# Routed expert layers on one core: the second layer of a tile two tiles behind its first, transposes two ahead, a whole PSUM bank per tile

## The chip, the cores and the metric

One core of a Trainium2 chip runs the whole program. The metric is the device time of one execution in microseconds (us). TensorE is PE in the profile, VectorE DVE, ScalarE ACT, GpSimd POOL, SyncE SP.

## What is computed

Two stages over 8192 tokens of 128 features, all in float32. The first is a graph layer (normalise, multiply with the adjacency, two dense layers, add the input). The second, which the change is about, sends each token to the best two of 8 experts:

```python
gate_logits = xf @ Wg + bg
top_w, top_i = jax.lax.top_k(gate_logits, TOP_K)      # TOP_K = 2
top_w = jax.nn.softmax(top_w, axis=-1)
w_dense = jnp.sum(jax.nn.one_hot(top_i, E) * top_w[..., None], axis=1)
for e in range(E):                                    # E = 8, D = 128, H = 512
    h = jax.nn.gelu(xf @ W1[e] + b1[e], approximate=False)
    out = out + w_dense[:, e:e + 1] * (h @ W2[e] + b2[e])
x = x + out                                           # xf is the layernorm of x
```

## The kernel before

Tokens are handled in 16 groups of 512 in the graph stage. As groups finish, POOL writes their rows with indirect DMAs (`dispatch`, L495) to two tables in HBM, sorted by expert, one table for the first choice and one for the second. The expert stage then walks over 142 tiles of 128 rows: 71 tiles of first choices (`TILES`), then 71 of second choices (`NT` is 142). Each tile belongs to one expert, whose number and first row stand in small tables that the engines read into registers.

The program is written out engine by engine, and every engine runs its own list in order; semaphores are the only link. For tile i:

- **SP** loads the tile's rows from HBM to place i % 16 of `slot_rows` (`load_slots`, L390 or L393), once the write of tile i - 16 has landed (`added`). From tile 79 on the rows come from the table `forwarded`, to which the first-choice tiles were written; SP first waits until the writes of all first-choice tiles have landed (L436). For the eight second-choice tiles 71 to 78, which are loaded earlier, it loads the first-choice result apart (`load_prior`, L399), two such loads behind each of the loads of tiles 79 to 82.
- **DVE** normalises the rows (`norm_slots`, L1134, `AHEAD` = 4 tiles ahead of the tile it closes), copies the expert's first-layer weights and biases to place i % 4 of `block_w` (`copy_block`, L1128, 128x644, three tiles ahead), and closes a tile: it adds the output bias to PE's result (L1219; L1229 for second choices) and multiplies by the token's weight and adds (L1223; L1237).
- **PE** turns the normalised rows (`turn`, a transpose, L720), does layer 1 (four 128x128 products, L727) and layer 2 (four products summed in one bank, L742).
- **ACT** copies the turned rows to SBUF (`copy_slots`, L858) and applies the gelu to the four pieces of layer 1 (`gelu`, L864).
- **POOL** writes the closed rows back with an indirect DMA (`write_tile`: L507 to `forwarded` for first choices, L511 to the output for second choices). It is also the engine that raises variances to the power -1/2 for the last group (L484) and that dispatches its rows.

PE's order in iteration i is turn(i + 1), layer 1 of i, layer 2 of i - 1. Layer 1 of a tile fills halves of PSUM banks: two pieces in a bank, three banks in rotation (`FH_BANKS`), so that the three banks hold one tile and a half. ACT starts the gelu of the first two pieces when the first half is done:

```python
for c in range(C):                                            # layer1(i), PE
    after(pe, gelu_ready, 2 * (2 * i + c // 2 - FH_BANKS + 1))
    ...
act.wait_ge(fh_done, 2 * i + c // 2 + 1)                      # gelu(i), ACT
```

`turn` and layer 2 have two banks each (`TURN_BANK`, `Y_BANK`), `slot_t` and `gelu_t` two buffers each. Layer 2 of tile i waits for the bias addition of tile i - 2 (`y_chain`), which empties its bank. The small steps that finish the last group (statistics of the second norm, gate, ranks, tables for the late tiles) are laced into the first 17 iterations of DVE's list.

## Time and profile before

| | |
|---|---|
| median of 3 runs | 521.77 us (519.33 to 522.0) |
| profiled execution, span | 521.4 us |
| PE busy | 473.0 us, 91% |
| DVE, ACT, POOL busy | 343.4, 302.9, 271.9 us |
| 142 transposes of the expert stage | first at 205.16 us, last at 510.59 us |

A line of the profile names the engine, the line of the kernel, the operation, what it writes and reads, the number of instructions merged in the line and, in square brackets, how long the engine had stood idle before it and what ended that wait. PE counts each float32 product of 128x128 as two matmuls, so layer 1 and layer 2 of a tile are 8 matmuls each; a transpose is one. "PEclk" is the granted clock of PE as a share of 2.4 GHz, 0.5 being its lower level of 1.2 GHz.

### The profile page before, as it was taken

The page shows a single profiled execution, that of the slowest core. Times are in us where ns is not written, and L with a number is a line of the kernel's source. Part 1 is how long each engine was busy: PE and PEld are TensorE (multiplying, and loading weights), DVE is VectorE, ACT ScalarE, POOL GpSimd, SP SyncE. Part 2 cuts the span into 40 slices and gives each one's busy share as a digit, 9 for nine tenths or more (in the row PEclk, how much of TensorE's full clock was granted, in tenths as well). Part 3 has the DMA queues.
Part 4 walks back from the last instruction along what each step waited for, and adds up shares of the span by engine and source line. Part 5 has one row for each costly group of instructions (what it writes and reads, how often), then busy time and mean ns, then how long its engine had stood idle before and what let it go on. Part 6 is the DMA issues. An engine that isn't in the chain of part 4 may idle for free.

```text
span 521.4 us, 13855 instructions
## 1 busy us (share of the span) xinstructions
PE 473.0 (91%) x3585; PEld 418.1 (80%) x3585; DVE 343.4 (66%) x1438; ACT 302.9 (58%) x942; POOL 271.9 (52%) x276
## 2 busy tenths in 40 slices
PE   8999989889988986869698999899997999999995
PEld 5678666667766755869697999899987999999995
DVE  5777767779766765556656666666645666677673
ACT  4475545556554333645455766677755766777663
POOL 3325556568666665356555454445435544455544
PEclk9999999999999989789899999999998999999999
DMA  7993333322222222134333433333044433334210
GB/s 213 375 312 99 97 85 78 77 78 69 67 69 79 71 75 69 39 96 121 93 102 100 126 118 116 114 86 110 20 120 124 137 96 102 109 109 107 84 36 12
DMA packets 50835, 54.61 MB, mean 105 GB/s; under 512 B 10249, under 2 KB 39474, under 8 KB 50760
## 3 DMA queue, kind: packets, MB, share of 16 engines
q1 hardware_dynamic: 42048, 35.14, 25.7%
q0 software_dynamic: 8240, 18.29, 10.1%
q8 instruction: 34, 0.56, 0.5%
q14 instruction: 41, 0.34, 0.3%
q10 hardware_dynamic: 472, 0.29, 0.2%
HBM read 33.56 MB, written 21.52 MB: 106 GB/s over the span
## 4 chain that ended last, share of the span: by engine, by line
PE 66%; issue 12%; POOL 8%; another core or an unknown queue 6%; DVE 4%; ACT 3%; POOLq 0%; DVEq 0%; ACTq 0%
PE ps L727 25%; PE ps L742 25%; PE ps L647 5%; POOL dispatched_rows L495 4%; PE ps L720 3%; PE ps L633 2%; PE ps L607 2%; ACT gelu_t L864 2%; POOL powers L484 1%; POOL powers L476 1%; PE ps L640 1%; PE ps L597 1%; POOL out_y L511 1%; ACT hidden L790 1%
## 5 line engine op out<-in xcount | busy, mean ns | idle before, releaser
L864 ACT ACTIVATE gelu_t<-ps,block_w 128x128 f32<-128x128 f32 x568 | 164.4, 374 | 49.1 <-PE ps L727 37.2
L727 PE MATMUL ps<-slot_t,block_w 128*128 128x128 f32 x1136 | 155.8, 281 | 13.6 <-ACT slot_t L858 10.8
L742 PE MATMUL ps<-experts,gelu_t 128*128 x1136 | 156.0, 281 | 11.0 <-ACT gelu_t L864 8.2
L727 PEld LDWEIGHTS ps<-slot_t,block_w 128*128 128x128 f32 x1136 | 142.6, 196 | 15.4 <-ACT slot_t L858 12.0
L742 PEld LDWEIGHTS ps<-experts,gelu_t 128*128 128x128 f32 x1136 | 141.9, 196 | 15.1 <-issue 15.0
L511 POOL DMA_INDIRECT out_y<-slot_rows x71 | 69.7, 981 | 74.4 <-DVE slot_rows L1237 40.1
L507 POOL DMA_INDIRECT forwarded_rows<-slot_rows x71 | 71.1, 1002 | 71.6 <-DVE slot_rows L1223 41.5
L495 POOL DMA_INDIRECT dispatched_rows<-payload,row_idx x80 | 82.6, 1032 | 24.8 <-issue 22.2
L633 PE MATMUL ps<-agg_r,w1b 128*128 128x512 f32 x128 | 62.7, 619 | 13.4 <-ACT hidden L790 10.8
L1128 DVE COPY block_w<-experts 128x644 f32 x142 | 72.9, 513 | 1.3 <-issue 1.3
L858 ACT COPY slot_t<-ps 128x128 f32<-128x128 f32 x142 | 38.1, 269 | 59.4 <-PE ps L720 36.5
L647 PE MATMUL ps<-w2e,hidden 128*128 128x136 f32 x512 | 67.5, 279 | 0.0
L647 PEld LDWEIGHTS ps<-w2e,hidden 128*128 128x128 f32 x512 | 63.0, 190 | 0.0
L1219 DVE TENSOR_TENSOR y_bias<-ps,block_w 128x128 f32<-128x128 f32 x71 | 20.7, 291 | 58.2 <-PE ps L742 35.5
L633 PEld LDWEIGHTS ps<-agg_r,w1b 128*128 128x128 f32 x128 | 22.5, 194 | 42.9 <-issue 20.5
L1229 DVE TENSOR_TENSOR slot_rows<-ps,block_w 128x128 f32<-128x128 f32 x71 | 20.7, 291 | 49.8 <-PE ps L742 27.6
L1134 DVE TENSOR_SCALAR slot_n<-slot_rows 128x128 f32<-128x128 f32 x142 | 49.8, 352 | 1.8 <-issue 1.4
L790 ACT ACTIVATE hidden<-ps,vec_cols 128x512 f32<-128x512 f32 x64 | 41.7, 689 | 10.0 <-PE ps L633 9.1
L720 PE MATMUL ps<-ident,slot_n 128*128 128x128 f32 x142 | 39.1, 276 | 0.0
L476 POOL TENSOR_TENSOR powers<-powers_in,neg_half 128x4 f32<-128x4 f32 x15 | 16.7, 1114 | 38.4 <-DVE powers_in L927 38.4
L484 POOL TENSOR_TENSOR powers<-powers_in,neg_half 128x8 f32<-128x8 f32 (+1 forms) x16 | 23.2, 1449 | 22.4 <-DVE powers_in L954 22.4
L640 PEld LDWEIGHTS ps<-ident_wg,xs_t 128*128 128x128 f32 x128 | 20.6, 190 | 14.3 <-issue 14.3
(152 smaller groups left out, 458.7 us busy)
## 6 DMA issues: line engine op xcount, KB each, us to landing
slot_rows<-forwarded_rows SPq DMA_DIRECT2D x63, 131.0 KB
slot_rows<-dispatched_rows SPq DMA_DIRECT2D x79, 67.0 KB
xs<-in_x SPq DMA_DIRECT2D x16, 256.0 KB, 6.9
xs_t<-in_x_t SPq DMA_DIRECT2D x16, 256.0 KB, 6.1
experts<-in_f_w SPq DMA_DIRECT2D x16, 256.0 KB, 5.2
slot_rows<-rrms_rows SPq DMA_DIRECT2D x13, 256.0 KB
adj_in<-in_adj_t SPq DMA_DIRECT2D x16, 128.0 KB, 6.5
dispatched_rows<-payload,row_idx POOLq DMA_INDIRECT x80
```

The costliest lines, as they stand in the source:

```text
L495: pool.indirect_dma_start(rows[k], bass.IndirectOffsetOnAxis(row_idx[:, g, j * TOP_K + k:j * TOP_K + k + 1], 0), payload[:, g * JT + j, 0: ...
L507: pool.indirect_dma_start(forwarded, place, slot_rows[:, r, :], None, bounds_check=DUMMY - 1, oob_is_err=False).then_inc(added[r], 16)
L511: pool.indirect_dma_start(out, token, slot_rows[:, r, WID:FWD], None, bounds_check=T - 1, oob_is_err=False).then_inc(added[r], 16)
L633: pe.matmul(bank(n % H_BANKS, 0, GROUP), w1b[:, c * P:(c + 1) * P], agg_r[:, s % 2, :], start=True, stop=True).then_inc(h_done, 1)
L647: mm = pe.matmul(x2_part(j), hidden[:, c, j * P:(j + 1) * P], w2e[:, c, :], start=False, stop=(c == C - 1))
L720: pe.transpose(bank(TURN_BANK + i % 2, 0, P), slot_n[:, i % (AHEAD + 1), :], ident[:]).then_inc(slots_turned, 1)
L727: mm = pe.matmul(bank((2 * i + c // 2) % FH_BANKS, c % 2 * SLOTS, SLOTS), block_w[:, i % BLOCKS, c * P:(c + 1) * P], slot_t[:, i % 2, :], ...
L742: mm = pe.matmul(bank(Y_BANK + i % 2, 0, P), gelu_t[:, i % 2, c, :], experts[:, bass.ds(at + (OW2 + c * P), P)], start=(c == 0), stop=(c = ...
L790: act.activation(hidden[:, c, :], ps[:, (C * s + c) % H_BANKS, :], ACT.Silu, scale=vec_cols[:, GRW + c:GRW + c + 1]).then_inc(hidden_ready, 1)
L864: act.activation(gelu_t[:, i % 2, c, :], ps[:, (2 * i + c // 2) % FH_BANKS, c % 2 * SLOTS:(c % 2 + 1) * SLOTS], ACT.Gelu, bias=block_w[:, ...
L1128: dve.tensor_copy(block_w[:, i % BLOCKS, :], experts[:, bass.ds(at, OW2)]).then_inc(block_ready, 1)
L1134: dve.tensor_scalar(slot_n[:, i % (AHEAD + 1), :], row[:, X2:WID], row[:, MEAN:MEAN + 1], row[:, RSTD:RSTD + 1], ALU.subtract, ALU.mult).t ...
```

## The change

- PE's order in iteration i becomes layer 1 of i, turn(i + 2), layer 2 of i - 2.
- Layer 1 of a tile goes to one whole bank, three tiles in three banks, with one wait before and one signal behind its four products; ACT waits for the whole tile before the first gelu. `slot_t` has 3 buffers (`TURNS`), `gelu_t` 4 (`GELUS`), laid over the room of `adj_in`, which the graph stage no longer needs.
- `AHEAD` is 6 and `BLOCKS` 6: rows are normalised six tiles ahead and weights copied five ahead.
- DVE's closing is split: the bias addition (`add_bias`, which empties the bank) comes first in an iteration, then the norm, the weight copy and the register load, and the multiplication by the weight (`close_first`, `close_second`) last. The steps for the last group move: its statistics go ahead of the loop, the others one to two iterations earlier.

```diff
-BLOCKS = 4
+BLOCKS = 6
-    AHEAD = 4
+    AHEAD, LAG, TURNS, GELUS = 6, 2, 3, 4
...
-        slot_t = sb("slot_t", [P, 2, SLOTS])
-        gelu_t = sb("gelu_t", [P, 2, C, SLOTS])
+        slot_t = sb("slot_t", [P, TURNS, SLOTS])
+        gelu_t = adj_in[:].rearrange("p r j n -> p (r j n)").rearrange("p (t c s) -> p t c s", t=GELUS, c=C)
...
             def layer1(i):
                 pe.wait_ge(slots_copied, i + 1)
                 pe.wait_ge(block_ready, i + 1)
+                after(pe, gelu_ready, C * (i - FH_BANKS + 1))
                 for c in range(C):
-                    after(pe, gelu_ready, 2 * (2 * i + c // 2 - FH_BANKS + 1))
-                    mm = pe.matmul(bank((2 * i + c // 2) % FH_BANKS, c % 2 * SLOTS, SLOTS),
+                    mm = pe.matmul(bank(i % FH_BANKS, c * SLOTS, SLOTS),
...
-                    if c % 2:
-                        mm.then_inc(fh_done, 1)
+                mm.then_inc(fh_done, 1)
...
-            layer1(0)
-            for i in range(1, NT):
+            for i in range(NT + LAG):
                 if i == LAST_RANKS:
                     prefix(G - 1)
-                if i + 1 < NT:
-                    turn(i + 1)
-                layer1(i)
-                layer2(i - 1)
-            layer2(NT - 1)
+                if i < NT:
+                    layer1(i)
+                if i + 2 < NT:
+                    turn(i + 2)
+                if i >= LAG:
+                    layer2(i - LAG)
...
             def gelu(i):
-                after(act, y_done, i - 1)
+                after(act, y_done, i - GELUS + 1)
+                act.wait_ge(fh_done, i + 1)
...
+            for i in range(4, AHEAD):
+                norm_slots(i)
+                copy_block(i - 1, expert_of(dve, i - 1))
+                if i == 4:
+                    stats2_of(G - 1)
+                    moments2_of(G - 1)
+            at = expert_of(dve, AHEAD - 1)
             for i in range(NT):
+                if i < TILES:
+                    add_bias(i, y_bias[:, i % 2, :])
+                else:
+                    add_bias(i, slot_rows[:, i % RING, X2:WID])
                 if i + AHEAD < NT:
                     norm_slots(i + AHEAD)
                 if TILES < i <= TILES + SECONDS:
                     dve.wait_ge(y_chain, i)
-                if i + 3 < NT:
-                    copy_block(i + 3, at)
+                if i + AHEAD - 1 < NT:
+                    copy_block(i + AHEAD - 1, at)
...
                 if i < TILES:
-                    finish(i)
-                else:
-                    take_second(i)
+                    close_first(i)
```

PE's list in the expert stage, one iteration, before (`slots_copied`, `gelu_ready` and `y_chain` are the semaphores of ACT's copies, ACT's gelus and DVE's bias additions):

```order
L720 MATMUL ps<-ident,slot_n 128x128 [waits slots_copied,slots_normed]
L727 MATMUL ps<-slot_t,block_w 128x128 [waits gelu_ready,block_ready,slots_copied]
L727 MATMUL ps<-slot_t,block_w 128x128 [waits gelu_ready] x3
L307 TENSOR_LOAD early_expert
L307 ISA x2
L742 ISA [waits y_chain,gelu_ready]
L742 MATMUL ps<-experts,gelu_t 128x128
```

and now:

```order
L728 MATMUL ps<-slot_t,block_w 128x128 [waits gelu_ready,block_ready,slots_copied]
L728 MATMUL ps<-slot_t,block_w 128x128 x3
L721 MATMUL ps<-ident,slot_n 128x128 [waits slots_copied,slots_normed]
L308 TENSOR_LOAD early_expert
L308 ISA x2
L742 ISA [waits y_chain,gelu_ready]
L742 MATMUL ps<-experts,adj_in 128x128
```

The transpose has moved behind layer 1, the waits inside layer 1 are gone, and `adj_in` is the room of `gelu_t`.

DVE's list from the end of the last but one group to the first tiles' closing, before (L946 is the statistics of the last group):

```order
L1009 CAST row_idx<-row_f 128x8
L307 TENSOR_LOAD early_expert
L307 ISA x2
L1134 TENSOR_SCALAR slot_n<-slot_rows 128x128 [waits slots_loaded4]
L1128 ISA
L1128 COPY block_w<-experts 128x644
L307 TENSOR_LOAD early_expert
L307 ISA x2
L1219 TENSOR_TENSOR y_bias<-ps,block_w 128x128 [waits y_done]
L1223 SCALAR_TENSOR_TENSOR slot_rows<-y_bias,slot_rows 128x128 [waits y_chain]
L946 BN_STATS stats<-payload 128x6 [waits x2_ready]
```

and now:

```order
L1129 COPY block_w<-experts 128x644
L947 BN_STATS stats<-payload 128x6 [waits x2_ready]
L947 BN_STATS stats<-payload 128x6 x3
L953 BN_AGGR payload<-stats 128x2 [waits ln2_chain]
L953 BN_AGGR payload<-stats 128x2 x3
L955 TENSOR_SCALAR powers_in<-payload 128x4 [waits ln2_chain]
L1135 TENSOR_SCALAR slot_n<-slot_rows 128x128 [waits slots_loaded5]
L308 TENSOR_LOAD early_expert
L308 ISA x2
L1129 ISA
L1129 COPY block_w<-experts 128x644
```

The statistics of the last group now stand ahead of the first wait for `y_done`, and one more norm and weight copy too.

## Rows read from the trace of the kernel before

**Rows 1.** The page: span; timeline, DVE before the first bias addition.
```profile
span 521.4 us, 13855 instructions
...
215.70 0.29 DVE L1219 TENSOR_TENSOR y_bias<-ps,block_w 128x128 f32<-128x128 f32 x1 [4.05 <-PE ps L742]
```

**Rows 2.** Stretches, transposes alone: from:to length, PE busy (xtransposes) PEld, PEclk, DMA.
```profile
223.00:242.40 19.40, 1.94 (x7) 0.97 (x7) 0.91 0.37 106
242.40:265.00 22.60, 2.06 (x7) 1.19 (x8) 0.85 0.34 98
265.00:285.80 20.80, 2.45 (x9) 1.23 (x9) 1.00 0.37 107
285.80:342.00 56.20, 7.36 (x27) 3.87 (x28) 1.00 0.40 116
342.00:389.40 47.40, 6.82 (x25) 3.59 (x26) 1.00 0.31 83
389.40:403.40 14.00, 1.24 (x4) 0.69 (x5) 0.88 0.42 117
403.40:510.50 107.10, 14.99 (x55) 7.86 (x56) 1.00 0.35 97
```

**Rows 3.** Timeline of one steady tile: start, duration, engine, line.
```profile
361.18 1.06 PE L727 MATMUL ps<-slot_t,block_w 128*128 128x128 f32 x8
361.27 0.29 DVE L1219 TENSOR_TENSOR y_bias<-ps,block_w 128x128 f32<-128x128 f32 x1 [0.56 <-PE ps L742]
361.38 0.27 ACT L858 COPY slot_t<-ps 128x128 f32<-128x128 f32 x1 [0.24 <-issue]
...
361.88 1.14 ACT L864 ACTIVATE gelu_t<-ps,block_w 128x128 f32<-128x128 f32 x4 [0.24 <-issue]
...
362.07 1.06 PE L742 MATMUL ps<-experts,gelu_t 128*128 x8
362.12 0.49 DVE L1128 COPY block_w<-experts 128x644 f32 x1
```

**Rows 4.** Waits of PE, 200 to 521 us: total, times, longest.
```profile
PE ps L727 <- ACT slot_t L858: 10.8, 5, 4.6
PE ps L742 <- ACT gelu_t L864: 8.2, 9, 2.3
```

**Rows 5.** Timeline around the stop at 229 us.
```profile
223.09 0.27 PE L720 MATMUL ps<-ident,slot_n 128*128 128x128 f32 x1
...
227.09 0.98 POOL L507 DMA_INDIRECT forwarded_rows<-slot_rows  x1 [0.30 <-issue]
229.15 0.29 DVE L1219 TENSOR_TENSOR y_bias<-ps,block_w 128x128 f32<-128x128 f32 x1 [5.89 <-remote]
229.19 0.27 ACT L858 COPY slot_t<-ps 128x128 f32<-128x128 f32 x1 [3.72 <-remote]
...
229.51 2.07 PE L727 MATMUL ps<-slot_t,block_w 128*128 128x128 f32 x8 [2.64 <-ACT slot_t L858]
```

**Rows 6.** Timeline, POOL's power for the last group.
```profile
219.23 1.08 POOL L484 TENSOR_TENSOR powers<-powers_in,neg_half 128x4 f32<-128x4 f32 x1 [6.10 <-DVE powers_in L954]
```

**Rows 7.** Timeline of PE, the stop at 257 us.
```profile
257.73 2.07 PE L742 MATMUL ps<-experts,gelu_t 128*128 x8 [2.27 <-ACT gelu_t L864]
```

**Rows 8.** Timeline from the last first-choice tile to the tiles that wait for it.
```profile
374.12 0.98 POOL L507 DMA_INDIRECT forwarded_rows<-slot_rows  x1 [0.92 <-DVE slot_rows L1223]
...
377.26 0.34 SPq L393 DMA_DIRECT2D slot_rows<-forwarded_rows  x1
...
380.43 0.34 DVE L1134 TENSOR_SCALAR slot_n<-slot_rows 128x128 f32<-128x128 f32 x1
...
391.53 1.24 PE L727 MATMUL ps<-slot_t,block_w 128*128 128x128 f32 x8 [1.75 <-ACT slot_t L858]
```

**Rows 9.** Timeline near the end: a closing and its write, no weight copy between.
```profile
515.57 0.35 DVE L1237 SCALAR_TENSOR_TENSOR slot_rows<-slot_rows 128x128 f32<-128x128 f32 x1
516.71 0.98 POOL L511 DMA_INDIRECT out_y<-slot_rows  x1 [0.74 <-DVE slot_rows L1237]
```

More of the change, by code:

```diff
@@ L741, in layer2 @@
                 for c in range(C):
-                    mm = pe.matmul(bank(Y_BANK + i % 2, 0, P), gelu_t[:, i % 2, c, :],
+                    mm = pe.matmul(bank(Y_BANK + i % 2, 0, P), gelu_t[:, i % GELUS, c, :],
                                    experts[:, bass.ds(at + (OW2 + c * P), P)],
@@ L856, in copy_slots @@
                 act.wait_ge(slots_turned, i + 1)
-                after(act, fh_done, 2 * (i - 1))
-                act.copy(slot_t[:, i % 2, :], ps[:, TURN_BANK + i % 2, 0:SLOTS]).then_inc(slots_copied, 1)
+                after(act, fh_done, i - TURNS + 1)
+                act.copy(slot_t[:, i % TURNS, :], ps[:, TURN_BANK + i % 2, 0:SLOTS]).then_inc(slots_copied, 1)
             def gelu(i):
-                after(act, y_done, i - 1)
+                after(act, y_done, i - GELUS + 1)
+                act.wait_ge(fh_done, i + 1)
                 for c in range(C):
-                    act.wait_ge(fh_done, 2 * i + c // 2 + 1)
-                    act.activation(gelu_t[:, i % 2, c, :],
-                                   ps[:, (2 * i + c // 2) % FH_BANKS, c % 2 * SLOTS:(c % 2 + 1) * SLOTS], ACT.Gelu,
+                    act.activation(gelu_t[:, i % GELUS, c, :],
+                                   ps[:, i % FH_BANKS, c * SLOTS:(c + 1) * SLOTS], ACT.Gelu,
                                    bias=block_w[:, i % BLOCKS, OB1 + c:OB1 + c + 1]).then_inc(gelu_ready, 1)
             copy_slots(0)
+            copy_slots(1)
             for i in range(NT):
@@ L871, in _ @@
                     tanh(G - 1)
-                if i + 1 < NT:
-                    copy_slots(i + 1)
+                if i + 2 < NT:
+                    copy_slots(i + 2)
                 gelu(i)
@@ L1214, in _, with add_bias, close_first @@
                     early_counts(1)
[L1216 to L1217 removed]
+            def add_bias(i, into):
                 dve.wait_ge(y_done, i + 1)
[L1219 removed]
+                dve.tensor_tensor(into, ps[:, Y_BANK + i % 2, 0:P],
                                   block_w[:, i % BLOCKS, OB2:OB2 + P], ALU.add).then_inc(y_chain, 1)
+            def close_first(i):
                 dve.wait_ge(y_chain, i + 1)
[L1222 removed]
+                row = slot_rows[:, i % RING, :]
                 dve.scalar_tensor_tensor(row[:, WID:FWD], y_bias[:, i % 2, :], row[:, WEIGHT:WEIGHT + 1],
                                          row[:, X2:WID], ALU.mult, ALU.add).then_inc(y_ready, 1)
[L1226 to L1230 removed]
             def close_second(i):
```

45 lines of the change are left out of this document (16 added, 29 removed).

## The prediction

> **What bounds the kernel now.** I read four views. The stretches of the expert stage, with the transposes alone, count tiles, one transpose each. From 342.0 to 389.4 us there are 25 tiles in 47.4 us, 1.896 us each, with no time lost [rows 2]. The timeline of such a tile shows why: layer 1 starts at 361.18, layer 2 0.89 us later, and 2 x 0.89 plus 0.11 for the transpose is 1.896 [rows 3]. PE is the bound there and no buffer can make that tile faster. The change removes no work from PE. So all that it can win is the time by which the other stretches exceed 1.896 us a tile:
>
> - 223.0 to 242.4: 7 tiles, 19.4 - 13.3 = 6.1 us
> - 242.4 to 265.0: 7 tiles, 9.3 us
> - 265.0 to 285.8: 9 tiles, 3.7 us
> - 285.8 to 342.0: 27 tiles, 5.0 us
> - 389.4 to 403.4: 4 tiles, 6.4 us
> - 403.4 to 510.5: 55 tiles, 2.8 us
>
> The sum is 33.3 us [rows 2], 6% of the span of 521.4 us [rows 1]. That is the ceiling.
>
> The waits of PE say what ended its idle time: nearly all of it is ACT, with the copy of the turned rows (10.8 us in 5 waits, of which 4.6 lie before the first tile) and with the gelu (8.2 us in 9) [rows 4]. But ACT is not short of time: in a steady tile it works 0.27 + 1.14 us of 1.896 [rows 3]. The timeline around one stop shows what it waited for. The transpose of 223.09 is over at 223.36 by its record, but ACT copies it at 229.19, and DVE starts the bias addition of the layer 2 before it at 229.15; both had been idle for 3.7 and 5.9 us [rows 5]. So PE's signals reached two engines some 6 us late, and together. I call this a late signal. In this trace it comes while POOL issues indirect DMAs in a row, 0.30 us apart, and ends about 1 us behind the last of them (227.09 + 0.98, then 229.15) [rows 5]. I take the coincidence as it stands; what the change must do is bridge the late signals.
>
> **How late a signal may be, before and now.** Three paths lead from PE over another engine back to PE. From the steady tile [rows 3]:
>
> - Gelu: layer 1 starts at 361.18, its gelus end at 361.88 + 1.14 = 363.02, and layer 2 of the same tile starts 0.89 + 0.89 + 0.11 + 0.89 = 2.78 us after 361.18, at 363.96. A signal may be 0.9 us late. Now two more blocks of 0.89 and a transpose lie between, 1.9 us. But the first gelu waits for the whole tile; I take half of layer 1's length, 0.5 us, for that. Room: 2.3 us.
> - Transpose: it runs 0.11 us before 361.18, its copy ends at 361.65, and layer 1 needs it one tile later, at 363.08. Room 1.4 us. Now it stands behind layer 1 and is needed one block of 0.89 later: 2.3 us.
> - Bank of layer 2: it starts at 362.07; its bias addition is due at 361.27 + 1.90 = 363.17, ends at 363.46, and layer 2 of two tiles on needs the bank at 362.07 + 3.79 = 365.86. Room 2.4 us, and the same now: there are still two banks, and the addition stands first in DVE's iteration instead of behind the weight copy, which matters only when DVE is behind.
>
> So the shortest room rises from 0.9 to 2.3 us. **Each stop gets 1.4 us shorter**, and one shorter than that vanishes, with the refill behind it.
>
> **The sum.** Stretch by stretch, what stays of the excess:
>
> - 403.4 to 510.5 and 285.8 to 342.0: small stops; 7.8 us become 0.
> - 265.0 to 285.8: 3.7 become 1.0.
> - 242.4 to 265.0: the stop that ends at 257.73 is the largest of three (idle 2.27 us there alone [rows 7]), and PE stands at its lower clock behind it: PEclk 0.85 is a mean over 22.6 us, so 0.15 x 2 x 22.6 = 6.8 us were at 1.2 GHz [rows 2]. With two stops shortened by 1.4 us, and a third and half of the slow clock gone, 9.3 become 5.0.
> - 223.0 to 242.4: here the burst itself should go. POOL waited 6.10 us, until 219.23, for the last group's variance, dispatched two more blocks of rows, and only then wrote the first tiles in a row [rows 6, 5]. The statistics now stand ahead of DVE's loop, where DVE was idle for 4.05 us before 215.70 [rows 1]: some 6 us earlier, so that POOL is free when tile 0 is closed. 6.1 become 0.5.
> - 389.4 to 403.4: two stops, one of them 1.75 us [rows 8], shortened to about 2 us with refill. To that comes a price of the change. Tile 79 can be loaded only when tile 70 is written: write 374.12, load 377.26, norm 380.43 at the latest [rows 8]. From layer 2 of tile 70 to the transpose of tile 79 there were 7 tiles on PE; now there are 5 and a layer 1. And the closing of tile 70 stands behind the norm and the weight copy: from the start of the addition to the end of the copy DVE takes 361.27 to 362.61, 1.34 us [rows 3], of which the closing's 0.35 [rows 9] moves out, so it starts at 0.99 instead of 0.33, 0.66 us later. Tile 79 keeps some 0.5 us of room; tiles 80 to 84, whose loads share SP's queue with the eight loads of first-choice results, come up to 1 us late. 6.4 become 3.0, between 1 and 6.
>
> Together 9.5 of 33.3 us stay: a gain of 23.8 us. Edits at nothing: the extra norm and weight copy ahead of the loop (0.34 + 0.49 us) lie in DVE's 4.05 us idle [rows 1], without which the first tile would be closed 0.8 us later; the room of `gelu_t` and the third `slot_t` add no instruction. SP's loads keep room elsewhere: with 16 places and a norm 6 tiles ahead, ten tiles (19 us) lie between a closing and the norm that needs its place, and write, load and norm took 380.43 - 374.12 = 6.3 us in the narrowest place [rows 8]; before it was twelve tiles. The tail behind the last layer 2 is the same work. 521.4 - 23.8 = 497.6; the median of the runs shown is 0.4 us above the profiled execution, so I say **498 us**.
>
> A rule is weighed for the later closing. The Trainium skill ("SBUF — State Buffer", section "SBUF: two separate sides") says that while DVE copies float32 from SBUF to SBUF, GpSimd cannot write the descriptors of its DMAs. By it, a write behind the weight copy would start sooner after its closing than one ahead of it, and the later closing would cost about 0.1 us where I count 0.66. The trace does not show that: in a steady tile the write starts 0.8 us behind the closing with the copy in between, and at the end of the program, with no copy, it starts 0.79 us behind it (515.57 + 0.35, then 516.71) [rows 9]. I keep 0.66.
>
> **Rivals.**
>
> 1. *Long signals leave less.* If PE's stop is set by the end of the late signal and not by its start, the transpose and the bank decide in each long stop, and these gain 0.9 us and nothing. For it: in rows 5 both engines got their signals together. Then the stretches at 223, 242, 265 and 389 us give back about 9 us of 25.5, the small stops 7: 521.4 - 16 = 505. Chance 0.17.
> 2. *All of it is bridged*, the slow clock too, and the loads at tile 79 come in time: 521.4 - 33.3 = 488. For it, the stretch of 47.4 us at full rate [rows 2]. Chance 0.06.
> 3. *Nothing is bridged*: late signals last until POOL has no closed tile left, so a PE that runs on feeds them, and each grows by what the buffers give. 521.4, plus the 1 us at tile 79: 522. The Trainium skill ("Perfetto Trace Analysis", section "Optimization Strategy") ties a shortage of buffers to a gap that repeats from tile to tile; by that rule there is none here, since 25 tiles in a row show no gap. Chance 0.07.
> 4. *Slower: longer bursts.* During a late signal PE now finishes up to two tiles more. DVE then closes three in a row and POOL issues three or more DMAs 0.30 us apart, where it issued two. The run of writes that ended at 228.07 [rows 5] lies in the stretch that lost 6.1 us, some 3 us for each of its two stops. With some ten such places at +2 us each and the ceiling's small stops not recovered: 521.4 + 20 - 10 = 531. This decides from the point at which most of POOL's runs hold four DMAs or more. Against it: DVE closes a tile in no less than about 1.4 us (the steps of rows 3), POOL needs 1.28 a DMA, so POOL nearly keeps pace. Chance 0.06.
>
> The forecast's own case has 0.64: 490 to 504 us.
>
> **Numbers.** The smallest difference that runs of this kernel can tell is about 0.5%, 2.6 us. The range of 8 in 10 takes the forecast's case and the first rival and leaves out the other three: 490 to 512 us. Faster by over 0.5% (under 519.2): the forecast, rivals 1 and 2 and part of 3, 0.90. Within it 0.04; slower 0.06.
>
> **What would show it.** In the profile after: the same 1.896 us a tile in full stretches; PE's two large waits on ACT at 8 to 10 us together, the 4.6 ahead of the first tile among them, instead of 19.0; late signals on ACT and DVE still there, with PE running on; POOL's power for the last group near 213 us and no run of four writes behind it; the transposes of tiles 79 to 84 with up to 1 us of idle time, and DVE's norm there waiting for a load. It is wrong if those two waits stay above 15 us, if POOL's runs of four or more DMAs multiply, or if the tiles behind 79 lose over 5 us.

## Result, and the profile after

The kernel with the change took 527.43 us (median of 4 runs, 525.13 to 529.79), the kernel before 521.88 us (4 runs). The ratio is 1.0123, with a 95% interval of 1.0073 to 1.0172: slower by 1.2%, where 4.6% faster was forecast. The profiled execution of the changed kernel has a span of 523.8 us (521.4 before [rows 1]) and took 525.72 us. An execution more than 1.5% above the fastest of its kernel counts as slow; the ratios leave it out, the medians don't.

The stretches of the expert stage, transposes alone, in the kernel after (columns as in [rows 2]; the stretch from 212 to 223 us, which [rows 2] leaves out, held 5 transposes before):

```profile
212.00:223.00 11.00, 2.06 (x7) 1.12 (x7) 0.89 0.27 78
223.00:242.40 19.40, 2.88 (x11) 1.43 (x10) 1.00 0.40 114
242.40:265.00 22.60, 2.11 (x7) 1.12 (x7) 0.85 0.33 100
265.00:285.80 20.80, 2.73 (x10) 1.42 (x10) 1.00 0.37 110
285.80:342.00 56.20, 7.04 (x26) 3.56 (x25) 1.00 0.36 110
342.00:389.40 47.40, 6.33 (x23) 3.29 (x23) 1.00 0.29 82
389.40:403.40 14.00, 1.32 (x4) 0.70 (x4) 0.76 0.42 120
403.40:513.00 109.60, 14.91 (x55) 7.74 (x54) 1.00 0.34 92
```

Against [rows 2] it gains in two places: 11 tiles instead of 7 from 223 to 242, 10 instead of 9 from 265 to 286. It loses where I had no loss: 26 tiles in 56.2 us (6.9 us over 1.896 each, 5.0 before) and 23 in 47.4 us, the stretch that had run at full rate (3.8 us over, 0 before). From 389 to 403 us there are 4 tiles as before, now with the clock at 0.76 (0.88 before).

The waits of PE from 200 to 520 us (total, times, longest), which answer to [rows 4]:

```profile
PE ps L728 <- ACT slot_t L858: 7.4, 3, 3.6
PE ps L742 <- ACT adj_in L864: 7.0, 15, 0.5
PE ps L721 <- DVE slot_n L1135: 5.2, 3, 3.8
```

The first two fell from 19.0 to 14.4 us, the third is new, and the wait on the gelus is now 15 short ones instead of 9. (`adj_in` is the room in which `gelu_t` now lies.) Where these short waits come from shows in the timeline of six microseconds in the stretch that lost:

```profile
306.66 0.29 DVE L1220 TENSOR_TENSOR y_bias<-ps,block_w 128x128 f32<-128x128 f32 x1 [2.58 <-PE ps L742]
...
307.81 0.28 DVE L1220 TENSOR_TENSOR y_bias<-ps,block_w 128x128 f32<-128x128 f32 x1
...
308.69 0.98 POOL L508 DMA_INDIRECT forwarded_rows<-slot_rows  x1 [2.74 <-DVE slot_rows L1226]
...
309.31 0.29 DVE L1220 TENSOR_TENSOR y_bias<-ps,block_w 128x128 f32<-128x128 f32 x1 [0.29 <-PE ps L742]
...
309.97 1.14 POOL L508 DMA_INDIRECT forwarded_rows<-slot_rows  x1 [0.30 <-issue]
...
311.41 0.98 POOL L508 DMA_INDIRECT forwarded_rows<-slot_rows  x1 [0.30 <-issue]
...
312.00 1.06 PE L742 MATMUL ps<-experts,adj_in 128*128 x8
312.19 0.27 ACT L858 COPY slot_t<-ps 128x128 f32<-128x128 f32 x1 [2.89 <-PE ps L721]
...
313.03 0.29 DVE L1220 TENSOR_TENSOR y_bias<-ps,block_w 128x128 f32<-128x128 f32 x1 [2.49 <-remote]
...
314.48 1.15 PE L742 MATMUL ps<-experts,adj_in 128*128 x8 [0.42 <-DVE y_bias L1220]
...
315.06 0.98 POOL L508 DMA_INDIRECT forwarded_rows<-slot_rows  x1 [2.66 <-DVE slot_rows L1226]
```

PE's signals are late until 306.66 at DVE. It then adds the bias of three tiles at 306.66, 307.81 and 309.31, POOL writes them 0.30 us apart from 308.69 on, PE's next signals are late until 312.19 at ACT and 313.03 at DVE, and it begins again. From 306.66 to 313.03 are 6.37 us for three tiles, 2.12 us each instead of 1.896. This cycle of threes fills most of 286 to 361 us and 411 to 455 us. From 200 us on POOL issues 26 runs of three or more DMAs with less than 0.45 us between the end of one and the start of the next; before there were 10.

The last first-choice tiles and what waits for them, answering to [rows 8]:

```profile
375.38 0.34 SPq L394 DMA_DIRECT2D slot_rows<-forwarded_rows  x1
...
377.51 0.35 DVE L1135 TENSOR_SCALAR slot_n<-slot_rows 128x128 f32<-128x128 f32 x1 [1.15 <-DMA slot_rows<-forwarded_rows]
...
393.40 0.98 POOL L512 DMA_INDIRECT out_y<-slot_rows  x1 [0.30 <-issue]
395.51 0.29 DVE L1220 TENSOR_TENSOR slot_rows<-ps,block_w 128x128 f32<-128x128 f32 x1 [5.24 <-remote]
...
396.11 0.48 PE L721 MATMUL ps<-ident,slot_n 128*128 128x128 f32 x1 [3.84 <-DVE slot_n L1135]
```

The norm of tile 79 waits for its load, and behind that POOL issues a run of six, at whose end PE stands for 3.84 us.

What was gained and lost cancels inside the expert stage. From the second layer of tile 0 to that of tile 141 both traced executions take 300.5 us: the kernel after is 6.5 us ahead by tile 10 (19.2 us instead of 25.7) and 8.4 by tile 30, then loses 4.7 up to tile 70 (85.5 us for 40 tiles instead of 80.8) and 4.0 from tile 70 to 90. The spans differ by 2.4 us, 1.4 ahead of that stretch and 1.0 behind it. The medians differ by 5.5 us; the rest of that lies between executions and is in neither trace.

### The profile page after: what moved, and what is told of

The parts are those of the page before. It is cut to its first block, busy times and chain, and to the rows that moved or that the text cites. A ratio compares the mean times of both kernels' runs of the same rounds, so it can differ in the third digit from the quotient of the medians.

```text
span 523.8 us, 13856 instructions
## 1 busy us (share of the span) xinstructions
PE 473.2 (90%) x3585; PEld 416.1 (79%) x3585; DVE 330.8 (63%) x1438; ACT 289.7 (55%) x942; POOL 272.5 (52%) x276
## 4 chain that ended last, share of the span: by engine, by line
PE 55%; issue 16%; POOL 12%; another core or an unknown queue 6%; ACT 5%; DVE 4%; DMA 1%; SPq 0%; POOLq 0%; DVEq 0%; ACTq 0%
PE ps L742 21%; PE ps L728 20%; POOL dispatched_rows L496 7%; PE ps L721 5%; ACT adj_in L864 3%; PE ps L634 3%; POOL powers L477 2%; PE ps L648 2%; POOL powers L485 2%; PE ps L608 1%; PE ps L598 1%; DVE sum_sq L926 1%; PE ps L641 1%; DVE slot_n L1135 1%
## 5 line engine op out<-in xcount | busy, mean ns | idle before, releaser
L742 PE MATMUL ps<-experts,adj_in 128*128 x1136 | 155.4, 281 | 10.9 <-ACT adj_in L864 7.0
L864 ACT ACTIVATE adj_in<-ps,block_w 128x128 f32<-128x128 f32 x568 | 164.1, 387 | 1.3 <-PE ps L728 0.6
L742 PEld LDWEIGHTS ps<-experts,adj_in 128*128 128x128 f32 x1136 | 140.5, 195 | 17.1 <-issue 17.0
L508 POOL DMA_INDIRECT forwarded_rows<-slot_rows x71 | 72.7, 1024 | 74.5 <-DVE slot_rows L1226 50.5
L512 POOL DMA_INDIRECT out_y<-slot_rows x71 | 71.5, 1007 | 76.8 <-DVE slot_rows L1234 45.9
L496 POOL DMA_INDIRECT dispatched_rows<-payload,row_idx x80 | 79.8, 997 | 24.3 <-issue 22.2
L1129 DVE COPY block_w<-experts 128x644 f32 x142 | 70.5, 497 | 1.7 <-issue 1.5
L1220 DVE TENSOR_TENSOR y_bias<-ps,block_w 128x128 f32<-128x128 f32 x71 | 20.6, 290 | 63.5 <-PE ps L742 50.1
```

The costliest lines, as they stand in the source:

```text
L496: pool.indirect_dma_start(rows[k], bass.IndirectOffsetOnAxis(row_idx[:, g, j * TOP_K + k:j * TOP_K + k + 1], 0), payload[:, g * JT + j, 0: ...
L508: pool.indirect_dma_start(forwarded, place, slot_rows[:, r, :], None, bounds_check=DUMMY - 1, oob_is_err=False).then_inc(added[r], 16)
L512: pool.indirect_dma_start(out, token, slot_rows[:, r, WID:FWD], None, bounds_check=T - 1, oob_is_err=False).then_inc(added[r], 16)
L742: mm = pe.matmul(bank(Y_BANK + i % 2, 0, P), gelu_t[:, i % GELUS, c, :], experts[:, bass.ds(at + (OW2 + c * P), P)], start=(c == 0), stop= ...
L864: act.activation(gelu_t[:, i % GELUS, c, :], ps[:, i % FH_BANKS, c * SLOTS:(c + 1) * SLOTS], ACT.Gelu, bias=block_w[:, i % BLOCKS, OB1 + c ...
L1129: dve.tensor_copy(block_w[:, i % BLOCKS, :], experts[:, bass.ds(at, OW2)]).then_inc(block_ready, 1)
```

## The experiments

To read them together I count, in each profiled trace, the start of layer 2 of tile 0, the time from there to tile 70, from tile 70 to 90 and from tile 90 to 141, and POOL's runs of three or more DMAs less than 0.45 us apart, from 200 us on. At 1.896 us a tile the three stretches would take 132.7, 37.9 and 96.7 us (the last a little less, because no layer 1 stands between the second layers at the end). The kernel before was run beside every batch of experiments, and a ratio is always to it in the same batch.

| kernel | median, us | ratio (95%) | tile 0 at | 0-70 | 70-90 | 90-141 | runs of 3+ |
|---|---|---|---|---|---|---|---|
| before | 521.88 | | 214.0 | 157.6 | 44.3 | 98.6 | 10 |
| after | 527.43 | 1.0123 | 215.4 | 153.9 | 48.3 | 98.3 | 26 |
| e1 after, spaced | 509.82 | 0.9810 (0.9732-0.9889) | 215.3 | 144.9 | 45.5 | 94.8 | 1 |
| e2 order of before | 520.12 | 1.0043 (1.0008-1.0079) | 213.6 | 148.8 | 47.3 | 100.3 | 11 |
| e3 closing at once | 519.08 | 0.9982 (0.9933-1.0030) | 215.4 | 146.8 | 48.2 | 98.3 | 17 |
| e4 before, statistics early | 512.26 | 0.9880 (0.9815-0.9945) | 213.2 | 148.5 | 44.4 | 98.0 | 12 |
| e5 before, spaced | 513.12 | 0.9783 (0.9721-0.9846) | 215.5 | 150.8 | 42.4 | 95.8 | 2 |
| e6 before, in threes | 563.32 | 1.0747 (1.0684-1.0810) | 215.9 | 172.8 | 50.1 | 114.5 | 45 |
| e7 after, half the pause | 535.93 | none | 216.7 | 159.0 | 48.7 | 105.5 | 36 |
| e8 before, e4 + e5 | 511.02 | 0.9738 (0.9679-0.9797) | 216.3 | 147.4 | 44.1 | 95.8 | 1 |
| e9 e2, norms 4 ahead | 515.96 | 0.9868 (0.9792-0.9945) | 212.7 | 150.8 | 46.1 | 97.6 | 10 |
| e10 before, spread | 508.96 | 0.9743 (0.9682-0.9803) | 213.1 | 142.4 | 43.1 | 95.8 | 2 |
| e11 after, spread | 507.11 | 0.9730 (0.9667-0.9793) | 214.7 | 139.7 | 41.5 | 95.0 | 2 |
| e12 e6, spaced | 520.77 | 1.0004 (0.9958-1.0051) | 212.8 | 153.9 | 41.6 | 102.1 | 2 |
| e13 after, norms 5 ahead | 574.27 | 1.2326 (1.2250-1.2402) | 189.4 | 199.2 | 54.9 | 137.1 | 5 |
| e14 e13, spread | 600.31 | 1.2886 (1.2823-1.2948) | 189.1 | 202.5 | 55.3 | 137.7 | 1 |
| e15 transposes one ahead | 467.05 | 1.0031 (1.0008-1.0054) | 189.9 | 133.0 | 39.1 | 94.6 | 5 |
| e18 after, again | 468.50 | 1.0071 (1.0044-1.0099) | 189.8 | 133.0 | 40.0 | 94.5 | 6 |
| e16 load first | 467.90 | 1.0065 (1.0040-1.0089) | 191.9 | 133.0 | 38.8 | 94.5 | 5 |
| e17 e13, load first | 482.20 | 1.0323 (1.0255-1.0390) | 192.8 | 141.5 | 41.0 | 99.8 | 5 |

The kernel before took 519.05 us beside e1 to e4, 525.05 beside e5 to e8 and 520.69 beside e9 to e12, but 465.46 us beside e13 to e15 and 464.30 beside e16 to e18: the last two batches found the machine in a condition without late signals, and are told apart below. The traced executions of e7 and e13 took 539.84 and 590.63 us, so their columns belong to those and not to the median.

### Are runs of POOL's DMAs the cause? (e1, e5, e6, e12, e7)

**e1** and **e5** put a dead instruction of POOL behind every write, which waits only for the one before it, in the kernel after and in the kernel before:

```diff
+                after(pool, pause_done, i)
+                pool.memset(pause[:], 0.0).then_inc(pause_done, 1)   # pause is 128x256
```

> The changed kernel with one GpSimd memset of 128x256 behind each write of a tile, so that two writes in a row start about 1.7 us apart instead of 1.28. Theory A (the late signals of PE come from runs of GpSimd's indirect DMAs 0.30 us apart, and the deeper pipeline keeps such runs going, three DMAs every 6.4 us): the cycle between 286 and 361 us goes, 26 tiles take about 50 us instead of 56, and the time falls by 8 to 20 us, to 508 to 518 us. Theory B (the cycle is the engines' own, from three buffers or banks that fill and empty together, and GpSimd only follows): the cycle stays, 6.4 us for three tiles, and the time is 527 us or, where GpSimd now holds back the ring of rows, more.

> The kernel before with the memset of 128x256 behind each write of a tile. Theory A (runs of GpSimd's DMAs make PE's signals late, in either kernel): it gains too, but less than the changed kernel did (3.1%), since it has few runs of three: 510 to 517 us. Theory C (only the changed kernel is hurt by runs; the stops of the kernel before have another cause): no change, 519 to 522 us.

Both came to 2% below the kernel before, e1 to 3% below the kernel it changes, with an instruction more per tile, and the runs went. In e1 two neighbouring writes of a busy stretch look like this:

```profile
304.46 1.02 POOL L510 DMA_INDIRECT forwarded_rows<-slot_rows  x1 [0.17 <-issue]
305.48 0.33 POOL L517 MEMSET pause<- 128x256 f32 x1
305.98 0.97 POOL L510 DMA_INDIRECT forwarded_rows<-slot_rows  x1 [0.17 <-issue]
```

1.52 us lie between their starts, instead of 1.28. The two kernels are equal within their intervals: with the runs gone, the deeper pipeline shows no gain. From tile 30 to 70 both take 76.7 us, where the kernel after took 85.5 and the kernel before 80.8; 40 tiles at 1.896 us are 75.8. But the late signals are not all gone. Bias additions that start over 1.5 us behind the recorded end of their second layer (0.04 us is usual) number 12 in the kernel before, 31 after, 11 in e1 and 10 in e5. Most of those left lie before tile 30, where the dispatches stand among the writes without a pause, and behind tile 76; some of the latter are DVE waiting for forwarded rows.

**e6** makes the runs by force in the kernel before: POOL waits until a group of three tiles is closed. **e12** is e6 with e5's pause.

```diff
-                pool.wait_ge(y_ready, i + 1)
+                last = TILES if i < TILES else NT
+                pool.wait_ge(y_ready, min(3 * (i // 3) + 3, last))
```

> The kernel before, but GpSimd waits for three closed tiles and then writes the three in a row: runs of three everywhere, with nothing else changed on the other engines. Theory A: each run makes PE's signals 2 to 3 us late, which this PE order cannot bridge; 47 runs at 0.5 to 1.5 us each: 535 to 570 us. Theory B (GpSimd only follows the other engines): the ring of 16 rows hides a write that comes two tiles later, and the time stays within 1% except behind tile 79: 522 to 526 us.

> The kernel before with POOL's writes held back and issued in threes, as in the grouped run that took 563 us, and now with the 256-column memset behind every write. The writes still come in threes, but about 1.5 us apart instead of 1.28. Theory A (what delays the releases is how close the transfers stand): most of the 38 us go, 513 to 525 us, a ratio of 0.98 to 1.005. Theory B (holding the writes back in threes costs by itself, through DVE or the buffers that come free late): still above 545 us, a ratio over 1.04.

e6 lost 7.5%, and 48 of its bias additions are late by that count. Its timeline shows the cycle of the kernel after, with the order and the buffers of before:

```profile
332.01 0.98 POOL L508 DMA_INDIRECT forwarded_rows<-slot_rows  x1 [3.42 <-DVE slot_rows L1224]
...
333.29 0.98 POOL L508 DMA_INDIRECT forwarded_rows<-slot_rows  x1 [0.30 <-issue]
...
334.58 0.98 POOL L508 DMA_INDIRECT forwarded_rows<-slot_rows  x1 [0.30 <-issue]
...
336.40 0.29 DVE L1220 TENSOR_TENSOR y_bias<-ps,block_w 128x128 f32<-128x128 f32 x1 [3.00 <-PE ps L743]
336.43 0.27 ACT L859 COPY slot_t<-ps 128x128 f32<-128x128 f32 x1 [2.62 <-PE ps L721]
...
336.75 1.24 PE L728 MATMUL ps<-slot_t,block_w 128*128 128x128 f32 x8 [0.83 <-ACT slot_t L859]
```

e12 still holds the writes back and issues them in threes, but 1.5 us apart. Nearly all of the loss against the kernel before is gone (1.0004), and 11 additions are late; against e5's 0.978 the grouping itself costs some 2%. So what makes most of the late signals is that the DMAs follow each other at 1.28 us, not that three come together. Whether the longer distance helps or the instruction between them is told apart only by e7, and weakly.

**e7** halves the memset (128x128) in the kernel after.

> The changed kernel with a memset of 128x128 instead of 128x256 behind each write: about half the extra distance. Theory A with a graded effect: between the changed kernel and its spaced form, a ratio of about 0.99 to 1.00 to the kernel before; if any instruction between two DMAs suffices, as 128x256 did: 0.98.

The starts in a run are then 1.37 us apart (307.26 and 308.63 in its timeline). Three of four executions took 535 to 540 us (the traced one has 36 runs of three or more) and one took 521.5 us, where the kernel before took 525.05, so no ratio is given, and whether 1.37 us is enough stays open. In the traced execution an instruction between the DMAs did not stop the cycle.

### Which part of the change makes the runs? (e4, e2, e3, e9, e13, e15)

**e4** is the kernel before with only the last group's statistics moved ahead of DVE's loop (`stats2_of(G - 1)` and `moments2_of(G - 1)`).

> The kernel before with one edit: the statistics and moments of the last group ahead of DVE's loop. By my reading the first stretch (223 to 242 us) loses its run of four writes and gains 5 to 6 us, as it did in the changed kernel: 516 us. If the gain there came from the deeper pipeline instead, nothing changes: 522 us.

It is 1.2% faster than before. This part of the change is good and explains most of the gain at 223 us: e4 has 10 transposes from 223 to 242.4 us, the kernel after 11 and the kernel before 7.

**e2** is the kernel after with the order of before on PE and ACT: `turn(i + 1)`, `layer1(i)`, `layer2(i - 1)`, and `copy_slots(i + 1)`. **e3** is the kernel after with `close_first(i)` directly behind `add_bias(i, ...)`. **e9** is e2 with the norms four tiles ahead and four block buffers.

> The changed kernel with PE's and ACT's order as before (transpose of i + 1, layer 1 of i, layer 2 of i - 1); banks, buffers, six tiles ahead and DVE's order stay changed. Theory A (the cycle needs PE's run of two tiles ahead): no cycle of three tiles, stops as in the kernel before, and with the last group's statistics early the first stretch keeps its gain: 514 to 520 us. Rival (what costs is the rows being wanted six tiles ahead and the later closing): the stops behind tile 79 stay, 523 us or more.

> The changed kernel with the closing of a first-choice tile directly behind its bias addition, ahead of norm and weight copy. It starts 0.6 to 0.7 us sooner, so tile 70 is written that much sooner and the loads of tiles 79 to 84 come 0.7 us sooner: a gain of about 1 us there by every theory. The cycle: if the runs of three come from three closings in a row, the spacing of closings (1.14 us now) does not change and the cycle stays: 525 to 527 us. If it goes, the later closing was part of it.

> The kernel with the change in which TensorE and ScalarE keep the order of before, and the norms run four tiles ahead again instead of six, with four block buffers. Theory A (late releases behind runs of POOL's transfers, and a price of its own for six norms ahead where the forwarded writes of tile 79 are waited for): from tile 70 to tile 90 the second matmuls take 44 to 45 us instead of 47.3, the whole is 2 to 4 us faster than with six ahead, a ratio to the kernel before of 0.995 to 1.000. Theory B (six norms ahead cost nothing; tile 79 is late by the writes alone): 47 us again from tile 70 to 90 and a ratio of 1.002 to 1.008.

e3 removes the delay of the closing and most of the loss: 17 runs instead of 26, a ratio of 0.998. e2 brings the number of runs back to 11 and 153.9 us to 148.8 from tile 0 to 70, but keeps 47.3 us from tile 70 to 90. e9 is where e4 is (0.987 and 0.988): what is left of the change in it (whole banks, the buffers, the split closing) costs nothing, within the 0.7% of the intervals, without the deeper order. Both theories put the gain of e9 over e2 between tile 70 and 90, where only 1.2 us lie; 2.7 us lie behind tile 90. So the six norms ahead cost 1.7% together with this order (by ratios from two batches), and most of it in a place that I did not expect and did not find a cause for.

**e15** takes only the transposes back to one tile ahead, **e13** has the norms five tiles ahead.

```diff
-BLOCKS = 6
+BLOCKS = 5
-    AHEAD, LAG, TURNS, GELUS = 6, 2, 3, 4
+    AHEAD, LAG, TURNS, GELUS = 5, 2, 3, 4
```

> The kernel with the change with the transposes one tile ahead as before on TensorE and ScalarE; the second layer stays two tiles behind. Theory A (the second layer two behind takes the wait on the gelus away, so that three second layers can follow each other at 1.1 to 1.5 us after a stop and DVE closes them in a row): the cycle stays, 15 runs of three or more, ratio 1.005 to 1.015. Theory B (the transposes two ahead make it): the time of the version with the order of before, 7 to 11 runs of three or more, ratio 1.000 to 1.006.

> The kernel with the change with the norms five tiles ahead instead of six and five block buffers; five is the least that its order allows. Theory A (the look-ahead of TensorE's order makes the runs of three, the depth of the norms only adds at tile 79): the cycle of three tiles stays, 15 runs of three or more, and the time is within 1% of the kernel with the change, a ratio to the kernel before of 1.003 to 1.015. Theory B (the depth of the norms, which lets DVE run ahead of the transposes, makes the runs): no more than 10 runs of three and a ratio of 0.985 to 0.998.

Neither question was answered, because no signal was late in this batch, but e13 showed something else, at 2.84 us a tile in its traced execution (590.63 us, the median is 574.27):

```profile
332.54 1.06 PE L728 MATMUL ps<-slot_t,block_w 128*128 128x128 f32 x8
332.74 0.29 DVE L1220 TENSOR_TENSOR y_bias<-ps,block_w 128x128 f32<-128x128 f32 x1 [1.67 <-PE ps L742]
332.95 0.34 DVE L1135 TENSOR_SCALAR slot_n<-slot_rows 128x128 f32<-128x128 f32 x1
...
333.44 0.27 PE L721 MATMUL ps<-ident,slot_n 128*128 128x128 f32 x1
...
334.44 1.15 PE L742 MATMUL ps<-experts,adj_in 128*128 x8 [0.73 <-ACT adj_in L864]
```

The norm that the transpose of 333.44 waits for stands on DVE behind the bias addition of the second layer just ended, and layer 2 starts a full microsecond after the transpose. The profile names the gelus as its releaser, but those in progress then are of two tiles later; the ones it reads are done. Between the two stands the register load with the expert's number, which PE's queue takes only when the transpose ahead of it has stopped waiting (0.51 us, and 1.09 us from the norm's release to layer 2). Layer 2, addition, norm, register load, layer 2: a closed ring. In the kernel after the norm is one tile earlier, and the ring is open. **e17** tests it by moving the load in front of the transpose; **e16** does the same to the kernel after:

```diff
+                if i >= LAG:
+                    at = expert_of(pe, i - LAG)
                 if i + 2 < NT:
                     turn(i + 2)
                 if i >= LAG:
-                    layer2(i - LAG)
+                    layer2(i - LAG, at)
```

> The kernel with norms five tiles ahead, which took 574 us at 2.84 us a tile, with the register load in front of the transpose. Theory A (closed ring: second layer, bias addition, norm, register load, second layer; 1.15 + about 0.6 + 1.1 = 2.85 us): without the load in the ring a tile takes 1.9 to 2.1 us and the kernel 470 to 495 us where the kernel before takes 465, 525 to 545 where it takes 520. Theory B (something else in the five-ahead kernel, as the buffers or ScalarE's order, sets 2.84 us): above 555 us again.

> The kernel with the change, TensorE's register load for the second layer moved from behind the transpose of two tiles ahead to in front of it. Theory A (a transpose that waits for its norm holds the register load back, and each such wait costs 1.1 us more): with late releases the time falls by 3 to 10 us against the kernel with the change in the same call; with releases on time nothing changes. Theory B (the load is always covered, the cycle comes from the releases alone): within 2 us of it in either case.

e17 took 482.2 us instead of 574.3, at 2.02 us a tile: the ring is shown. It is still 3.2% above the kernel before, and e16, with six norms ahead, only 0.65%, so five ahead cost something without the load too. e16 took the time of e18, so with signals on time the load costs the kernel after nothing; whether it does with late signals wasn't tried.

### Do the dispatches cost the same? (e8, e10, e11, e14)

**e8** joins e4 and e5. **e10** and **e11** put the pause behind the late dispatches too, leave it out in the last eight tiles, and place the four dispatches of the last group and three second choices three tiles apart (11, 14, 17 and 20; 23, 26 and 29), in the kernel before (with e4's edit) and after. **e14** is the same on e13.

```diff
-                if LAST_FIRSTS <= i < LAST_FIRSTS + JT:
-                    dispatch(G - 1, i - LAST_FIRSTS, 0)
+                if LAST_FIRSTS <= i < LAST_FIRSTS + 3 * JT and (i - LAST_FIRSTS) % 3 == 0:
+                    dispatch(G - 1, (i - LAST_FIRSTS) // 3, 0)
+                    rest()
```

> The kernel before with both edits that helped: the last group's statistics ahead of the loop and the memset of 128x256 behind each write. If the two gains are of different stretches they add: ratio 0.97 to 0.98, 506 to 510 us. If they both live on the runs of the first stretch: 0.985 to 0.99.

> The kernel before with the statistics of the last group early, the 256-column memset on POOL behind every write and every dispatch except in the last eight tiles, and the three late dispatches and the three second choices put three tiles apart. Theory A (each run of POOL's transfers close together costs TensorE up to 3 us): tiles 10 to 30, where the dispatches stand between the writes, take 40 to 46 us instead of 49.5, and the whole is 3 to 5 us below the version with the memset behind the writes alone: a ratio to the kernel before of 0.962 to 0.970. Theory B (the early stretch is bound by the dispatches' own work and by the layout of the routing, not by how close they stand): 49 us or more there and a ratio of 0.972 to 0.980, or above that if the later dispatches hold up tiles behind 30.

> The same three edits on the kernel with the change (its statistics stay where the change has them). Theory A (with the releases on time the deeper look-ahead gains nothing, and six norms ahead cost 2 to 4 us behind tile 79): the time of the spread kernel before plus 0 to 4 us, a ratio to the kernel before of 0.965 to 0.978. Theory B (the deeper look-ahead does gain once the releases are on time): at least 3 us below the spread kernel before, a ratio under 0.962.

> The kernel with the change, norms five ahead, with the memset behind every write and dispatch except in the last eight tiles and the late dispatches three tiles apart. Theory A (spaced transfers leave hardly a run, and the depth of the norms then only costs at tile 79): 505 to 508 us, ratio to the kernel before 0.966 to 0.975, as with six ahead. Theory B (the depth costs by itself everywhere): at least 3 us below the version with six ahead, ratio under 0.967.

From tile 10 to 30 the second layers take 42.4 us in e10, where e8 took 49.5, and the span fell by 3.5 us; the ratios, from two batches, do not tell them apart. Part of what was won is lost at the end. e10's last write is issued at 497.1 us and has landed by 499.3 (SP's last wait for it is over then), but POOL's closing instruction, a DRAIN, ends only at 507.4. From the last write to the end of the span lie 10.5 us in e10, e11 and e14, the three that leave out the memset in the last eight tiles, and 3.2 to 3.3 us in all other traces. Why is open. Without these 7.3 us e10 would take some 501.7 us, a ratio near 0.963 by this estimate, where 0.962 to 0.970 was expected. e11 is as fast as e10 within the interval. At 507.11 us it is the fastest version in the usual condition of the machine, 2.7% below the kernel before. Its 41.5 us from tile 70 to 90 also speak against a fixed price of six norms ahead. e14 is held by e13's ring and tells nothing of its question.

### The machine without late signals (e18)

> The kernel with the change, unchanged, a second time. If the kernel before takes some 520 us in this call (releases late): again a ratio of 1.007 to 1.017 and the cycle of three tiles. If it takes some 465 us (releases on time): theory A (the change loses only through late releases) 0.998 to 1.006, no cycle, one tile per 1.90 us; theory B (the change costs by itself, through the norms six ahead or the order) over 1.008.

In these two batches the kernel before took 464 to 465 us instead of 519 to 525, and the graph stage too was faster: tile 0 starts at 190 us instead of 214. The first stage has this wait of ACT on a signal from PE in the kernel after, as its first profile names it:

```profile
ACT agg L815 <- remote: 31.7, 9, 4.1
```

and in e18, the same program:

```profile
ACT agg L815 <- PE ps L598: 9.9, 16, 1.4
```

The trace of e18 has no wait at all on "remote"; the trace of after has 126 us of them in 50 places, over all engines, that of the kernel before 92 us in 39. And POOL's runs cost nothing there. From 212.6 to 245.6 us POOL issues 25 DMAs 0.30 us apart, writes and dispatches, and PE turns 18 tiles in 33 us; from 345 on, 57 in 110:

```profile
212.50:245.50 33.00, 4.91 (x18) 2.58 (x18) 1.00 0.47 134
345.00:455.00 110.00, 15.54 (x57) 8.16 (x57) 1.00 0.37 103
```

In the whole of e18 one bias addition is late by the count used above. Within that run of 25 DVE starts the bias addition at 231.04, as soon as the second layer is over by its record (229.95 + 1.06):

```profile
229.95 1.06 PE L742 MATMUL ps<-experts,adj_in 128*128 x8
230.09 0.98 POOL L508 DMA_INDIRECT forwarded_rows<-slot_rows  x1 [0.30 <-issue]
231.04 0.29 DVE L1220 TENSOR_TENSOR y_bias<-ps,block_w 128x128 f32<-128x128 f32 x1 [0.61 <-PE ps L742]
```

So closely spaced DMAs delay PE's signals only in one condition of the machine, and this condition was there in 12 experiments and in the first comparison. What makes it is open: the kernels are the same, and the traces do not show it. It is not the chip, for chips 6 and 8 were each met in both conditions (e5 to e8 and e13 to e15; e1 to e4 and e16 to e18). Nor is it the clock of PE: up to 190 us the granted clock is 0.99 in the kernel before, 1.00 in the kernel after and 1.00 in e18. It is also not told apart whether the signals come late or PE's work itself ends later than recorded, since the profile models the ends of matmuls.

In this condition the change is still slower, by 0.7% (3.3 us at a median of 464.3), with nothing to bridge. Up to 2 us of it can lie at tile 79, in the stops of the timeline of PE:

```profile
334.81 1.15 PE L742 MATMUL ps<-experts,adj_in 128*128 x8 [0.28 <-DVE slot_rows L1220]
...
336.70 0.27 PE L721 MATMUL ps<-ident,slot_n 128*128 128x128 f32 x1
337.05 1.15 PE L742 MATMUL ps<-experts,adj_in 128*128 x8
...
339.81 1.15 PE L742 MATMUL ps<-experts,adj_in 128*128 x8 [0.60 <-ACT adj_in L864]
```

Tiles 70 to 90 take 40.0 us there, 2.1 more than at full rate; DVE's norm waits 5.3 us in five places for forwarded rows. From tile 0 to 70 it runs at 1.90 us a tile. Another microsecond seems to lie at the end: from the end of the last second layer to the end of the span e18 takes 6.9 us, the kernel after 6.8 and the kernel before 5.8 (with late signals). The kernel before was not traced in this condition, so neither place is certain.

## Why the prediction was wrong

**The ceiling and its places** (33.3 us by stretches) were read rightly for that trace, but it was a ceiling for that condition of the machine alone. At 1.896 us a tile PE is the bound: in e18 it runs at this rate from tile 0 to 70.

**"Each stop gets 1.4 us shorter"** is the step that failed. It took the number and the length of the late signals as given and let the change bridge them. Most of them are made by POOL's runs (e6, e12), and POOL's runs are made by what PE and DVE do behind a late signal: PE's second layers stand ready, DVE closes three tiles at once (307.54, 308.66 and 310.18 in the cycle shown), and POOL, which needs 1.28 us for each, issues all three 0.30 us apart. Deeper look-ahead feeds this ring: with the order of before (e2) the runs are 11, with it 26. 26 runs instead of 10, and 6.37 us for three tiles, took what the bridging gave. The two waits fell to 14.4 us, not to 8 to 10, and the small stops, which I set from 7.8 to 0, grew: 6.9 + 3.8 us from 286 to 389 alone, where it had been 5.0. A smaller slip lies in the sum: I went from span to time with 0.4 us, but in the profiled execution after 1.9 us lie between them (523.8 and 525.72).

**Rival 4** had the mechanism and a chance of 0.06. I set its threshold at runs of four or more and argued that DVE's 1.4 us a tile let POOL nearly keep pace. Runs of four or more hardly multiplied (7 instead of 6). Runs of three are enough, as e6 shows, and POOL makes one while it keeps pace: DVE's closings lie 1.12 and 1.52 us apart. So two of my signs of being wrong, waits over 15 us and runs of four, never came, though the forecast was wrong; the third did, for the stretch behind tile 79 still loses 6.4 us. The rival's price of 2 us a place was too high: 0.7 us for three tiles. And I took the coincidence in [rows 5] "as it stands" where it should have been asked whether spacing the DMAs would do what the change was to do; e1, e5 and e12 say so.

**Early statistics** (6.1 to 0.5 us at 223): right. POOL's power for the last group starts at 213.65 without a wait, predicted near 213:

```profile
213.65 1.04 POOL L485 TENSOR_TENSOR powers<-powers_in,neg_half 128x4 f32<-128x4 f32 x1
```

e4 prices it alone at 1.2%.

**Stretch 389 to 403** (6.4 to 3.0 us): it stayed at 6.4, with 0.76 of the clock, and tile 79's norm waits for its load, as foreseen. The place was right, the price of a microsecond too low: from tile 70 to 90 it is 4 us more than in the kernel before with late signals, and with signals on time about 2 us more than at full rate.

**The closing 0.66 us later** was a term of the tile-79 price only. e3 shows that it matters everywhere: 1.4% between e3 and the kernel after (ratios from two batches), with 17 runs instead of 26. How the delay makes runs is not shown.

**Edits at nothing**: right for layout and buffers (e9 against e4), and nearly so for two tiles of lag with signals on time (e15, 0.3%). "The tail behind the last layer 2 is the same work" was not: from the end of the last second layer to the end of the span lie 6.8 to 7.1 us in the traces with two tiles of lag and no pause (after, e3, e13, e15 to e18) and 5.0 to 5.8 in those with one tile of lag (before, e2, e4, e9). With two, three second layers end the program in a row, and POOL issues the last five writes 1.28 us apart.

**Rival 3, the rule on bubbles from the Trainium skill** ("Perfetto Trace Analysis", "Optimization Strategy"): it says that the same gap repeating for a stretch can mean too few buffers. I read it the other way round, no such gap, no shortage, which the page does not say. The trace agrees with that reading: there was nothing to win in the 25 tiles of [rows 2], and in e18, with signals on time, nothing is won in the whole stage.

## What to carry to other kernels

Before buffers are added against late signals, ask what makes them late, and whether a deeper pipeline makes more of it: a stall that one's own bursts cause isn't a fixed length to be bridged. Cheap tests are to space the suspected transfers with a dead instruction and to bunch them by force. When a stage is moved two tiles behind, move every producer that stands behind it by as much (the norm five ahead closed a ring that six left open), and keep register loads in front of instructions that may wait.

## What the runs showed of the hardware

- In one condition of the machine PE's signals to ACT and DVE, by the recorded ends of its work, arrive 2 to 6 us late while POOL issues indirect DMAs 1.28 us apart from start to start: 7.5% with runs of three by force. At 1.5 us apart the same grouping loses nothing (1.0004, e12), and tiles 30 to 70 run at 1.92 us each (e1, e5), though other signals stay late. At 1.37 us it is undecided (e7).
- In another condition, in two batches, a run of 25 such DMAs delays nothing (e18), and the same program takes 11% less (464.3 instead of 519 to 525 us). Two chips showed both conditions.
- PE's register load that stands behind a waiting transpose starts only when the wait ends, and costs 1.1 us up to the next product: 2.84 us a tile against 2.02 with the load ahead of it (e13, e17).
- In the three traces in which all writes but the last eight had a memset behind them, the span ended 10.5 us behind the start of the last write, held by POOL's closing DRAIN, and in all others 3.2 to 3.3 us (e10, e11, e14 against the rest).
